# Edge-record scatters of a two-layer graph network kernel: the pacing by SyncE's answers is taken out, the pacing by TensorE's products stays

## The chip, the cores and the metric

One core of a Trainium2 chip runs the whole program in one launch. The metric is device time in microseconds, the median of three runs. PE is TensorE (its weight loads are shown as PEld), DVE is VectorE, ACT is ScalarE, POOL is GpSimd and SP is SyncE. A name with q behind it (SPq, POOLq) is the instruction queue of that engine.

## The reference, cut to what matters

Two layers work on N = 6250 nodes with 256 features and 200000 edges. Each layer adds three things to x: a sum over edges, a linear attention over all nodes, and a feed-forward part.

```python
xn = _layernorm(x)
x = x + _L0_gnn_ref(xn, src, dst, ...) + _L0_mix_ref(xn[None], ...)[0]
x = x + _L0_ffn_ref(_layernorm(x)[None], ...)[0]
xn = _layernorm(x)
x = x + _L1_gnn_ref(xn, edge_weight, W, b, src, dst) + _L1_mix_ref(xn[None], ...)[0]
x = x + _L1_ffn_ref(_layernorm(x)[None], ...)[0]
# _L0_gnn_ref: softmax-weighted sum of x[s] over the edges of each target d
# _L1_gnn_ref: segment_sum((x @ W)[edge_col] * edge_val, edge_row) + b
```

The first edge sum goes by `dst`, and the edges arrive sorted by it. The second goes by `src`, and for it the kernel has to bring the edges into another order itself.

## The kernel before

The nodes stand in 50 blocks of 125. Two blocks are a chunk, so a pass over all nodes has 25 chunks (NC = 25). The kernel runs in stages, with all engines joined between them: sort_edges (places of the edges are counted), first_layer (layer 0's norm, projections, attention), edge_softmax (layer 0's edge sum with gathers), second_layer (layer 0's feed-forward, layer 1's projections and attention), edge_sums (layer 1's edge sum with gathers), norm_and_route, and the last feed-forward part.

The second order of the edges is made by scatters. An edge is a record of three words. `Turns` writes them from SBUF to the DRAM tensor `records1`, 128 records with one indirect DMA on POOL (L585). There are 46 turns of 34 scatters, 1564 in all. A turn has two halves of SLOT = 17 scatters, and each half has its own buffer (`slot_rec`, `slot_pos`). One turn (34 scatters) runs in sort_edges, FIRST_TURNS = 18 turns (612 scatters) in first_layer, and 27 turns (918 scatters) in second_layer. In both layers the scatters run beside TensorE's work and nothing in the layer needs them. The end of the stage does: POOL waits there for all of its scatters to land.

Three waits stand ahead of a scatter:

- `filled` (L577), once for each half: SP has loaded the half's 17 columns of records and positions (L549, L550). SP issues these loads when the scatters that used this buffer before have landed (`sent[h]`).
- `beat` (L582), ahead of 21 of the 34 scatters of a turn. PE's products in first_layer and second_layer increment it, and before the loop POOL adds `lead` to it itself (L574): `Turns("a", turns, 21, 40)` in first_layer and `Turns("b", turns, 21, 50)` in second_layer. Scatter n of turn i needs a count of 21 i + floor(21 n / 34) + 1. So the scatters may run ahead of PE by 40 or 50 counts, and one count is 34/21 scatters.
- `seen` (L583), ahead of each scatter. This is the answer of SP. POOL increments `issued` ahead of each scatter (L584). SP waits in its function `follow` for each of these increments, and increments `seen` for each (L541). It starts with AHEAD = 2 answers given, so scatter j waits for the answer to scatter j - 2. SP gives the answers in the order of its own program: between them stand its waits for `sent[h]` and its issues of the loads for the next half.

first_layer runs two passes of 25 chunks on PE. In the first pass (keys, values and small projections; L774, L782, L790, L794) a chunk gives 7 counts. In the second pass (queries, messages, feed-forward; L815, L827, L840, L848) it also gives 7. L774 and L815 leave 8 matmul records for a chunk. DVE does the counting of places (`Places.blocks`, L217 to L227) during the first pass. SP may only load positions that are already spilled, and waits for `spilled[i]` between batches of turns.

second_layer begins with the selection of the top rows: BITS + 2 = 18 rounds between PE (L1175) and DVE, each a product that waits for DVE's counts and gives them back summed. Its passes then give 8 counts per chunk (feed-forward, L1200), 3 (keys, values, products; L1233) and 10 (queries and messages; L1255, L1282, L1289, L1304, L1315).

Of the kernel before, what the change touches and what calls it, by code (L numbers as in the profile page):

```python
# [35 lines left out]
LAG = 4  # L36
AHEAD = 6
RW = 3
# [6 lines left out]
SLOT = 17  # L45
# [27 lines left out]
def settle(pool, cell, settled, before):  # L73

    pool.wait_ge(settled, before)
    pool.tensor_tensor(cell, cell, cell, ALU.add).then_inc(settled, 1)  # L76
# [25 lines left out]
def gps_kernel(nc, A, out):  # L102
# [3 lines left out]
    def sem(name):  # L106

        held = nc.semaphore(name)
        phase_sems.append((held, held.__enter__()))
        return phase_sems[-1][1]  # L110
# [35 lines left out]
    with ctx:  # L146
# [376 lines left out]

        class Turns:

            AHEAD = 2

            def __init__(self, name, turns, beats=0, lead=0):
                self.at, self.turns, self.beats, self.lead = moved[0], turns, beats, lead
                self.filled = [sem(f"{name}_filled{h}") for h in range(2)]  # L530
                if beats:
                    self.beat = sem(name + "_beat")
                self.settled, self.issued, self.seen = (sem(f"{name}_{x}") for x in ("settled", "issued", "seen"))
                moved[0] += 2 * SLOT * turns

            def sp(self, sp, first, n):

                def follow(i, h, a, b):
                    with loop(sp, b - a) as j:
                        sp.wait_ge(self.issued, i * (2 * SLOT) + (h * SLOT + a + 1) + j)  # L540
                        sp.sem_inc(self.seen, 1)  # L541

                def turn(i, k):
                    for h in range(2):
                        at = self.at + first * 2 * SLOT + h * SLOT
                        cols = bass.ds(i * (2 * SLOT) + at, SLOT)
                        if not (isinstance(i, int) and self.at + first == 0):
                            sp.wait_ge(sent[h], i * (16 * SLOT) + 8 * (self.at + first * 2 * SLOT))
                        sp.dma_start(slot_rec[:, h, :, :], spill_rec[1][:, cols, :]).then_inc(self.filled[h], 16)  # L549
                        sp.dma_start(slot_pos[:, h, :], spill_pos[1][:, cols]).then_inc(self.filled[h], 16)  # L550
                        if h:
                            follow(k, 0, 4, SLOT)
                        elif not (isinstance(k, int) and k == 0):
                            follow(k - 1, 1, 4, SLOT)
                        follow(k, h, 0, 4)

                if first == 0:
                    sp.sem_inc(self.seen, self.AHEAD)
                    turn(0, 0)
                    if n > 1:  # L560
                        first = 1
                        with loop(sp, n - 1) as i:
                            turn(i, i + 1)
                        first = 0
                elif n:
                    with loop(sp, n) as i:
                        turn(i, i + first)
                if first + n == self.turns:
                    follow(self.turns - 1, 1, 4, SLOT)

            def pool(self, pool):

                if self.beats:
                    pool.sem_inc(self.beat, self.lead)  # L574
                with loop(pool, self.turns) as i:
                    for h in range(2):
                        pool.wait_ge(self.filled[h], i * 32 + 32)  # L577
                        settle(pool, cell[0:1, 0:1], self.settled, i * 2 + h)
                        for j in range(SLOT):
                            n = h * SLOT + j  # L580
                            if self.beats and (n * self.beats // (2 * SLOT) > (n - 1) * self.beats // (2 * SLOT)):
                                pool.wait_ge(self.beat, i * self.beats + n * self.beats // (2 * SLOT) + 1)  # L582
                            pool.wait_ge(self.seen, i * (2 * SLOT) + h * SLOT + j + 1)  # L583
                            pool.sem_inc(self.issued, 1)  # L584
                            pool.indirect_dma_start(  # L585
                                out=rec_d[1], out_offset=bass.IndirectOffsetOnAxis(ap=slot_pos[:, h, j:j + 1], axis=0),
                                in_=slot_rec[:, h, j, :], in_offset=None).then_inc(sent[h], 16)
                for h in range(2):
                    pool.wait_ge(sent[h], 8 * (self.at + 2 * SLOT * self.turns))
# [1300 lines left out]
        def edge_softmax(edge):  # L1890
# [4 lines left out]
            with ExitStack() as c:  # L1895
# [32 lines left out]
                with nc.Block() as block:  # L1928
# [73 lines left out]
                    def _(act):  # L2002
# [19 lines left out]
                        def body(t, s):  # L2022
                            d, x = s % 2, step(t, s)
                            if near(t, s, AHEAD):
                                step_records(act, *near(t, s, AHEAD))
                            if near(t, s, 3):
# [8 lines left out]

                        for i in range(AHEAD):
                            step_records(act, 0, i)
# [398 lines left out]
```

## Time and profile before

| | us |
|---|---|
| median of three runs | 8288.19 |
| lowest and highest run | 8277.54 and 8334.47 |
| the profiled execution | 8300.19 |
| its span | 8298.5 |
| PE busy | 5030.9 (61%) |
| POOL busy | 4735.0 (57%) |
| DVE busy | 3712.8 (45%) |
| L585, the scatters, x1564: busy | 1573.5 |
| L585: POOL idle just before them | 942.9 |

first_layer's part with scatters runs from about 200 to 1215 us of the span, second_layer's from about 3981 to 5560 us. A PE that is busy for 61% of the span isn't at its limit there, since the matmuls are pipelined. Idle time of POOL ahead of a scatter is shared out by the semaphore event that came last before it, so a wait that ended by PE's count is often shown as one for SPq L541, because SP's answer comes just behind it.

### The profile page before, as it was taken

Reading aid. Unit: us, or ns where it says so; the run is one execution under the profiler, and the core shown is the slowest. Engines: PE = TensorE matmul, PEld = TensorE weight load, DVE = VectorE, ACT = ScalarE, POOL = GpSimd, SP = SyncE. Lnnn points to the kernel's source line nnn. Section 1 sums busy time; section 2 is a strip of 40 time slices with the busy share of each in tenths; the row PEclk is TensorE's granted clock in tenths of the full one; section 3 lists DMA queues with packets and bytes.
Section 4 is the critical chain, followed back from the end, with each engine's and each line's share of the span. In section 5 each row is a group of like instructions: output and inputs, shape, how many; then the busy total and the mean of one; then the engine's idle time right before and its main releaser. Section 6 shows DMA issues by size and latency. Waiting matters only on the chain. (4 is left out here: it accounts for less than half of the span.)

```text
span 8298.5 us, 129786 instructions
## 1 busy us (share of the span) xinstructions
PE 5030.9 (61%) x23474; PEld 3877.8 (47%) x23475; DVE 3712.8 (45%) x14369; ACT 1845.1 (22%) x4706; POOL 4735.0 (57%) x5589
## 2 busy tenths in 40 slices
PE   0464666666666667776288777654445444444499
PEld 0353544545554545555266666543333333333377
DVE  6463444444555555555554424433333333333445
ACT  6111333333333333333122222210000000000044
POOL 2576646665555555555566556656666666666500
PEclk9886767787778888888689988877777777777799
DMA  3100003333333333333100000013333333333200
GB/s 87 34 4 6 3 13 89 90 89 87 84 85 84 81 81 84 82 82 80 36 3 4 20 17 3 3 32 91 91 91 91 91 91 91 91 91 92 74 25 18
DMA packets 505323, 495.45 MB, mean 60 GB/s; under 512 B 374862, under 2 KB 402135, under 8 KB 504407
## 3 DMA queue, kind: packets, MB, share of 16 engines
q0 software_dynamic: 200192, 432.72, 19.1%
q1 hardware_dynamic: 154712, 33.52, 2.2%
q10 hardware_dynamic: 150271, 27.46, 1.9%
q8 instruction: 66, 1.08, 0.1%
q14 instruction: 82, 0.67, 0.0%
HBM read 463.03 MB, written 30.23 MB: 59 GB/s over the span
## 5 line engine op out<-in xcount | busy, mean ns | idle before, releaser
L1847 POOL DMA_INDIRECT XN<-table,XN x3128 | 2984.5, 954 | 985.6 <-issue 917.4
L585 POOL DMA_INDIRECT records<-slot_rec,slot_pos x1564 | 1573.5, 1006 | 942.9 <-SPq L541 531.2
L2159 PE MATMUL gcn_psE<-XN,gcn_pE 128*125 x3520 | 1125.0, 484 | 1213.3 <-DVE gcn_pE L2175 922.9
L2159 PEld LDWEIGHTS gcn_psE<-XN,gcn_pE 128*125 128x125 f32 x3520 | 825.8, 243 | 1512.5 <-issue 1352.2
L1978 PE MATMUL gat_psE<-XN,gat_pE 128*125 x3520 | 1112.8, 470 | 190.2 <-ACT gat_pE L2034 171.2
L1978 PEld LDWEIGHTS gat_psE<-XN,gat_pE 128*125 128x125 f32 x3520 | 784.3, 234 | 351.9 <-issue 206.2
L2187 DVE TENSOR_TENSOR X<-X,gcn_psE 125x256 f32 x440 | 184.3, 419 | 1537.3 <-remote 1077.6
L76 POOL TENSOR_TENSOR cell<-cell 1x1 int32<-1x1 int32 x874 | 162.7, 186 | 1174.7 <-remote 505.4
L2241 ACT ACT_TABLE_LOAD x1 | 1.3, 1283 | 2345.0 <-PEq L118 2345.0
L1970 PE MATMUL gat_psP<-ident,XN 125*128 125x125 f32 x1760 | 325.7, 316 | 324.3 <-ACT gat_sc L2030 211.2
L2175 DVE TENSOR_SCALAR gcn_pE<-iota_n,gcn_lk,gcn_rec 128x125 f32<-128x125 f32 x1760 | 502.8, 362 | 16.0
L1970 PEld LDWEIGHTS gat_psP<-ident,XN 125*128 125x128 f32 x1760 | 241.1, 165 | 466.8 <-ACT gat_sc L2030 253.5
L2072 DVE COPY gat_mo<-edge_m 125x1 f32 x440 | 67.7, 154 | 871.2 <-remote 641.6
L1962 PE MATMUL gat_psS<-XN,gat_kTs 32*125 32x128 f32 x3520 | 255.6, 364 | 312.8 <-DVE gat_df L2078 202.7
L2061 DVE TENSOR_SCALAR gat_pen<-gat_psT,iota_p 125x512 f32<-125x512 bf16 x440 | 329.4, 749 | 172.4 <-ACT XN L2010 101.6
L2034 ACT ACTIVATE gat_pE<-gat_psP 128x500 f32<-128x500 f32 x440 | 257.8, 586 | 587.7 <-PE gat_psP L1970 283.7
L1962 PEld LDWEIGHTS gat_psS<-XN,gat_kTs 32*125 32x125 f32 x3520 | 166.5, 215 | 412.7 <-issue 245.6
L2019 ACT ACTIVATE XN<-XN 128x100 f32 x440 | 128.1, 291 | 883.1 <-issue 876.5
L2029 ACT ACTIVATE XN<-XN,gat_nm 125x512 f32<-125x512 f32 x440 | 310.8, 706 | 9.0 <-issue 9.0
L2073 DVE CUSTOM_DVE_ANT_0 XN<-gat_psS,gat_pen 125x512 f32<-125x512 f32 x440 | 304.3, 692 | 0.0
L1200 PE MATMUL b_bank<-room,b_wf 128*128 128x250 f32 x800 | 217.1, 432 | 79.3 <-ACT room L1354 46.8
L1200 PEld LDWEIGHTS b_bank<-room,b_wf 128*128 128x128 f32 x800 | 171.1, 223 | 123.8 <-ACT room L1354 51.4
(454 smaller groups left out, 8178.0 us busy)
## 6 DMA issues: line engine op xcount, KB each, us to landing
XN<-table,XN POOLq DMA_INDIRECT x3128
records<-slot_rec,slot_pos POOLq DMA_INDIRECT x1564
XN<-records SPq DMA_DIRECT2D x782, 6.0 KB
gat_rec<-records ACTq DMA_DIRECT2D x440, 6.0 KB
gcn_rec<-records ACTq DMA_DIRECT2D x440, 6.0 KB
table<-XN ACTq DMA_DIRECT2D x5, 1250.0 KB
table<-room ACTq DMA_DIRECT2D x25, 250.0 KB
out_x<-X SPq DMA_DIRECT2D x25, 250.0 KB
```

The costliest lines, as they stand in the source:

```text
L585: pool.indirect_dma_start(out=rec_d[1], out_offset=bass.IndirectOffsetOnAxis(ap=slot_pos[:, h, j:j + 1], axis=0), in_=slot_rec[:, h, j, :] ...
L1200: last = pe.matmul(psH[i % 2][:, 0:TOK], wf1[:, j, i * P:(i + 1) * P], xT[:, j, :], start=(j == 0), stop=(j == KF - 1))
L1847: pool.indirect_dma_start(out=rows_t[:, s, j, :], out_offset=None, in_=table, in_offset=bass.IndirectOffsetOnAxis(ap=rec_g[:, s, j, 1:2].b ...
L1962: last = pe.matmul(psS[0:B, j, :], kTs[r, d, :], qT[r, d, :], start=True, stop=True)
L1970: last = pe.transpose(psP[:, j * B:(j + 1) * B], pT[:, d, j * P:(j + 1) * P], ident[0:B, 0:B])
L1978: last = pe.matmul(psE[d][0:B, 0:D], pE[:, d, j * B:(j + 1) * B], rows_t[:, slot_of(g), j, 0:D].rearrange("p a w -> p (a w)"), start=(j == ...
L2029: act.activation(pT[:, d, :], S[:, d, :], ACT.Exp, bias=nm[:, d:d + 1], scale=SC, accum_out=rs[:, d:d + 1])
L2034: act.activation(pE[:, d, :], psP[:, 0:SUB * B], ACT.Copy).then_inc(p_done, 1)
L2061: dve.tensor_scalar(pen[:, d, :], psB[0:B, :], iota_p[0:B, 0:1], -BIG, ALU.not_equal, ALU.mult).then_inc(pen_done, 1)
L2073: st(dve.tensor_tensor_reduce(out=S[:, d, :].rearrange("p (j n) -> p j n", j=SUB), in0=psS[0:B, :, :], in1=pen[:, d, :].rearrange("p (j n) ...
L2159: last = pe.matmul(psE[d][0:B, 0:D], pE[:, d, j, :], rows_t[:, slot_of(g), j, :].rearrange("p a w -> p (a w)"), start=(j == 0), stop=(j == ...
L2175: last = dve.tensor_scalar(pE[:, d, j, :], iota_n[:, :], lk[:, d, j:j + 1], rec_t[:, s, j, 2:3], ALU.is_equal, ALU.mult)
```

## The change

`Turns` loses `AHEAD`, `issued`, `seen` and `follow`. SP's part of a turn is now only the wait for `sent[h]` and the two loads of each half. POOL's part keeps the waits for `filled` and `beat`. Behind each wait for `beat` (21 in a turn) it now increments a new semaphore, `paced`, that nothing waits for. The leads stay 40 and 50. sort_edges' turn has no beats, so its 34 scatters now wait for `filled` alone. Nothing else differs between the two kernels.

```diff
--- before.py
+++ after.py
@@ -523,24 +523,17 @@
 
         class Turns:
 
-            AHEAD = 2
-
             def __init__(self, name, turns, beats=0, lead=0):
                 self.at, self.turns, self.beats, self.lead = moved[0], turns, beats, lead
                 self.filled = [sem(f"{name}_filled{h}") for h in range(2)]
                 if beats:
-                    self.beat = sem(name + "_beat")
-                self.settled, self.issued, self.seen = (sem(f"{name}_{x}") for x in ("settled", "issued", "seen"))
+                    self.beat, self.paced = sem(name + "_beat"), sem(name + "_paced")
+                self.settled = sem(name + "_settled")
                 moved[0] += 2 * SLOT * turns
 
             def sp(self, sp, first, n):
 
-                def follow(i, h, a, b):
-                    with loop(sp, b - a) as j:
-                        sp.wait_ge(self.issued, i * (2 * SLOT) + (h * SLOT + a + 1) + j)
-                        sp.sem_inc(self.seen, 1)
-
-                def turn(i, k):
+                def turn(i):
                     for h in range(2):
                         at = self.at + first * 2 * SLOT + h * SLOT
                         cols = bass.ds(i * (2 * SLOT) + at, SLOT)
@@ -548,25 +541,13 @@
                             sp.wait_ge(sent[h], i * (16 * SLOT) + 8 * (self.at + first * 2 * SLOT))
                         sp.dma_start(slot_rec[:, h, :, :], spill_rec[1][:, cols, :]).then_inc(self.filled[h], 16)
                         sp.dma_start(slot_pos[:, h, :], spill_pos[1][:, cols]).then_inc(self.filled[h], 16)
-                        if h:
-                            follow(k, 0, 4, SLOT)
-                        elif not (isinstance(k, int) and k == 0):
-                            follow(k - 1, 1, 4, SLOT)
-                        follow(k, h, 0, 4)
-
-                if first == 0:
-                    sp.sem_inc(self.seen, self.AHEAD)
-                    turn(0, 0)
-                    if n > 1:
-                        first = 1
-                        with loop(sp, n - 1) as i:
-                            turn(i, i + 1)
-                        first = 0
-                elif n:
+
+                if self.at + first == 0:
+                    turn(0)
+                    first, n = 1, n - 1
+                if n:
                     with loop(sp, n) as i:
-                        turn(i, i + first)
-                if first + n == self.turns:
-                    follow(self.turns - 1, 1, 4, SLOT)
+                        turn(i)
 
             def pool(self, pool):
 
@@ -580,8 +561,7 @@
                             n = h * SLOT + j
                             if self.beats and (n * self.beats // (2 * SLOT) > (n - 1) * self.beats // (2 * SLOT)):
                                 pool.wait_ge(self.beat, i * self.beats + n * self.beats // (2 * SLOT) + 1)
-                            pool.wait_ge(self.seen, i * (2 * SLOT) + h * SLOT + j + 1)
-                            pool.sem_inc(self.issued, 1)
+                                pool.sem_inc(self.paced, 1)
                             pool.indirect_dma_start(
                                 out=rec_d[1], out_offset=bass.IndirectOffsetOnAxis(ap=slot_pos[:, h, j:j + 1], axis=0),
                                 in_=slot_rec[:, h, j, :], in_offset=None).then_inc(sent[h], 16)
```

## Rows read from the trace of the kernel before

**Rows 1.** The page: the span, PE's line, and the group of the scatters

```profile
span 8298.5 us, 129786 instructions
...
PE 5030.9 (61%) x23474; PEld 3877.8 (47%) x23475; DVE 3712.8 (45%) x14369; ACT 1845.1 (22%) x4706; POOL 4735.0 (57%) x5589
...
L585 POOL DMA_INDIRECT records<-slot_rec,slot_pos x1564 | 1573.5, 1006 | 942.9 <-SPq L541 531.2
```

**Rows 2.** Waits in 535 to 865 us, SP's and POOL's: us, times, longest

```profile
SPq L541 <- POOLq L584: 1.0, 4, 0.3
...
POOL records L585 <- issue: 53.5, 159, 2.1
POOL records L585 <- SPq L541: 51.3, 53, 4.7
```

**Rows 3.** The same waits of SP in 865 to 1180 and in 4130 to 5500 us

```profile
SPq L541 <- POOLq L584: 107.9, 94, 4.5
...
SPq L541 <- POOLq L584: 382.1, 323, 24.8
```

**Rows 4.** L585 alone by windows: stretch, length, POOL busy (scatters), PE clock, DMA, GB/s

```profile
200.00:535.00 335.00, 217.11 (x204) 0.88 0.11 27
430.00:535.00 105.00, 83.77 (x70) 0.87 0.04 5
535.00:682.00 147.00, 95.21 (x99) 0.70 0.10 8
682.00:865.00 183.00, 120.09 (x124) 0.68 0.03 3
865.00:1180.00 315.00, 182.08 (x187) 0.74 0.03 3
3970.00:4100.00 130.00, 83.82 (x81) 0.53 0.18 52
```

**Rows 5.** L774 alone by windows, PE and PEld (8 records are a chunk)

```profile
270.00:385.00 115.00, 22.47 (x48) 14.93 (x48) 0.78 0.10 24
385.00:430.00 45.00, 11.59 (x40) 8.03 (x40) 0.96 0.02 4
430.00:535.00 105.00, 23.88 (x64) 15.79 (x64) 0.87 0.04 5
535.00:665.00 130.00, 22.21 (x48) 14.91 (x48) 0.73 0.06 4
```

**Rows 6.** L815 alone by windows, PE and PEld (8 records are a chunk)

```profile
680.00:865.00 185.00, 18.45 (x64) 14.60 (x64) 0.68 0.03 3
865.00:1180.00 315.00, 35.72 (x136) 30.41 (x136) 0.74 0.03 3
```

**Rows 7.** Timelines of PE, ACT, DVE and POOL, 650 to 674 us: start, length, idle before

```profile
650.18 0.96 POOL L585 DMA_INDIRECT records<-slot_rec,slot_pos  x1 [0.30 <-issue]
651.53 2.09 PE L646 MATMUL a_bank<-room 125*128 125x129 f32 x8 [4.22 <-issue]
...
659.30 18.28 ACTq L890 DMA_DIRECT2D spill_pos<-room  x1
...
669.83 0.18 DVE L655 COPY a_kvd<-a_bank 32x32 f32<-32x32 f32 x1 [10.56 <-remote]
...
673.37 0.96 POOL L585 DMA_INDIRECT records<-slot_rec,slot_pos  x1 [3.20 <-SPq L541]
```

**Rows 8.** Timeline of PE, the 18 rounds of the selection (1st, 4th, 10th, 18th)

```profile
4058.46 0.58 PE L1175 MATMUL b_bank<-b_cnt,ones 125*125 125x3 f32 x2 [85.89 <-issue]
...
4077.01 0.58 PE L1175 MATMUL b_bank<-b_cnt,ones 125*125 125x3 f32 x2 [10.65 <-issue]
...
4097.26 0.58 PE L1175 MATMUL b_bank<-b_cnt,ones 125*125 125x3 f32 x2 [4.44 <-DVE b_tot L1476]
...
4115.12 0.58 PE L1175 MATMUL b_bank<-b_cnt,ones 125*125 125x3 f32 x2 [1.57 <-DVE b_v L1496]
```

**Rows 9.** Waits of ACT's L1403, which reads L1255's product: us, times

```profile
  remote: 120.9, 21
```

## The prediction

> **What bounds the kernel now.** The page first: PE is busy for 61% of the span, and POOL stands idle for 942.9 us ahead of its scatters, 531.2 of them put down to SP's answers [rows 1]. That is the sum the change seems to be after. Two questions come before it: did an answer end this idle time, and does anything wait for the scatters?
>
> The waits of SP and POOL, cut by stretch, answer the first. From 865 to 1180 us SP itself waits 107.9 us for POOL's `issued` [rows 3]. SP is there ahead of POOL, and what holds POOL can only be PE's count. From 4130 to 5500 us it is the same, with 382.1 us [rows 3]. From 535 to 865 us SP waits for POOL for 1.0 us in all [rows 2]. There SP is the late one and its answers hold POOL: 51.3 + 53.5 us in 212 gaps [rows 2], and with 0.30 us for a gap without a wait [rows 7] this leaves 105 - 64 = 41 us of pauses in 223 scatters.
>
> The counts say the same. By 535 us PE has done (48 + 40 + 64) / 8 = 19 chunks [rows 5], 133 counts, and with the lead 173. 204 scatters have run [rows 4], and the next needs 6 x 21 + 1 = 127. POOL has 46 counts in hand. By 865 us it has issued 427 and the next needs 12 x 21 + 11 + 1 = 264, and PE has given 175 + 8 x 7 = 231 [rows 6] and the lead 40. The hand is nearly empty, and it stays so to the last scatter. The lead in second_layer is 50 counts, 81 scatters, and 81 is what runs by 4100 us [rows 4].
>
> The second question: the scatters end before PE does in both stages, so POOL's idle time is off the path. The path is PE's chain with DVE and ACT. But the scatters press on it. At 651.53 us PE starts the last key-value sums, 2.09 us of work, and DVE, which waits for them, starts at 669.83 us, after 10.56 us of idle time [rows 7]. An issue of a DMA on ACT takes 18.28 us in the same stretch [rows 7]. Nothing of this is work. The semaphore updates of the products arrive late while POOL issues at its full rate, 0.96 + 0.30 = 1.26 us for a scatter [rows 7], and they arrive when POOL has paused for a few microseconds (here the 3.20 us ahead of 673.37 [rows 7]). The selection in second_layer measures it. Its last 8 rounds, after POOL's lead is spent, take (4115.12 - 4097.26) / 8 = 2.23 us each. The 9 rounds before that, beside the scatters, take 38.8 / 9 = 4.3 us each, and one gap in them is 10.65 us [rows 8]. Where a scatter takes longer the pressure is gone: from 430 to 535 us one comes each 1.5 us, and PE makes 8 chunks in 105 us, 13.1 us each. From 535 us on it takes 130 / 6 = 21.7 us for a chunk [rows 4, 5].
>
> **The change part by part.** Taken out on POOL: 1564 increments and waits; on SP: 1564 waits and increments. They run in the queues beside a scatter of 0.96 us and take nothing off the path. Added: 945 increments of `paced` on POOL, hidden in the same way, and at most some tens of ns each behind a beat wait if not. SP comes to its wait for `sent[h]` sooner, so the loads of the next half (two issues each) come as early as now or earlier; behind them in SP's queue only the wait for spilled positions stands, which is set by DVE.
>
> What is left is what the answers do to POOL's rhythm. An answer is a semaphore update too. When updates are late it is late as well, POOL stops, and the backlog clears. Without it POOL goes on as long as it has counts in hand, and loses nothing by PE's being late.
>
> First layer, to 385 us: POOL has few counts over; a change of some microseconds either way, taken as 0. From 385 to 535 us nothing changes, since positions and DVE set the pace. At 535 us POOL has 46 counts, 46 x 34/21 = 74 scatters, and now issues them at 1.26 us: 94 us in which PE's chain gets little done, to 629 us. From then on each scatter waits for PE's count. In this regime, 865 to 1180 us, a chunk takes 315 / 17 = 18.5 us with 11 scatters [rows 4, 6]. The 6 chunks left of the first pass take 111 us, so the pass ends at about 740 us instead of 665, and 75 us are lost. The 8 chunks of the second pass that now take 183 / 8 = 22.9 us each take 18.5, and 35 us come back. Net +40 us. Two bounds. If the waits for the buffers (one each 17 scatters) let PE do two chunks within the burst, 37 us come off: +3. If a chunk of the first pass takes 20 us and one of the second 19, the net is +94 + 120 - 130 - 31 = +53. I take +25, nearer to the middle, because the trace has no run of scatters without answers and so no row for a complete standstill.
>
> Second layer, selection: POOL's 81 scatters end some 4 us sooner. If PE stands still until then (4095 us) with 15 rounds left, these end at 4095 + 15 x 2.23 = 4128 us instead of 4115: +13. If the rounds run as now, -4. I take +8. The rest of the stage is held by counts already [rows 3], and stays: 0. The sum is 8300 + 25 + 8 = 8333 for an execution like the profiled one. This one stood 12 us over the median, so 8320 us for the median.
>
> DMA: Bandwidth & Descriptors of the Trainium skill (section Anatomy of one DMA) says that the DMA engines wait for no semaphore, and that every wait happens at the issuing sequencer. By that nothing but POOL's own waits bounds what is outstanding; the trace agrees in so far as POOL's pauses are what ends the late updates [rows 7].
>
> **The rivals.**
> *Nothing changes (chance 0.26).* The answers only follow POOL, and PE loses to the scatters what it loses to them in any rhythm: the number of scatters stays 612 and 918. For it: the time that the burst costs comes back, as the +3 above shows. It gives 8300 - 12 + 0 = 8288, from -10 to +10. SBUF: State Buffer of the Trainium skill (section SBUF: two separate sides) has a rule on this side: only GpSimd's and VectorE's shared port contends, and PE and ACT wait for no one. By it the scatters could not hold PE in any rhythm and the sum would be 0. The 10.56 and 18.28 us of idle and issue time beside dense scatters [rows 7] speak against reading it so widely, for they are no access to SBUF.
> *The bursts grow everywhere (0.16).* Slower by more than 1%. Also where counts are few, an answer now cuts a run of scatters short. ACT waits 120.9 us in 21 chunks for products of L1255 that PE has long issued [rows 9], 5.8 us each. If a run is longer by two scatters, 2.5 us, in each of the second layer's 75 chunks and the first layer's last 17, this is 92 x 2.5 = 230 us at most; with half of it on the path, and the 33 above, 8288 + 33 + 115 = 8436. It decides from 0.6 us per chunk on. Against it: SP is ahead in these stretches [rows 3], so its answers are seldom the last.
> *The answers are part of the load (0.10).* Each scatter carries two more semaphore updates and a loop of SP. Without them 1.26 us per scatter may be slow enough that no backlog forms. Then first_layer's 14 chunks between 535 and 865 us run at 18.5 us or less: 330 - 259 = 71 us saved, and the selection's 18, in all 8288 - 89 = 8199. Against it: two updates beside the landing of a DMA on 128 partitions are little.
>
> **How the numbers follow.** The forecast has 0.48: 8320 us, alone 8285 to 8350. A measurement of this kernel can tell about 1% (83 us) from no change. Slower by over 1% are the rival of growing bursts and the tail of the forecast: 0.16 + 0.02. Faster by over 1% is most of the last rival: 0.08. Within 1%: 0.46 + 0.26 + 0.02 = 0.74. The range leaves out half of each outer rival: 8255 to 8395 us.
>
> **What would show it.** In the profile after: POOL's idle ahead of L585 in 535 to 640 us falls to 0.30 us a scatter, with runs of some 17 or more. The chunks of L774 stand nearly still there, and from about 640 us on come each 17 to 20 us; L815 begins at about 740 to 760 us instead of 682. The rounds of L1175 bunch behind POOL's 81st scatter. Stages without records scatters keep their lengths. Wrong would be: L774 at its present 21.7 us or faster right through the burst (the last rival, or none), or chunks of L1255 that take longer than now (the rival of growing bursts).

## The result, and the profile after

The changed kernel takes 8331.2 us (median of 20 runs, 8307.5 to 8373.4) against 8302.7 us of the kernel before (20 runs, 8269.7 to 8334.5). The ratio is 1.0041, with a 95% interval of 1.003 to 1.0052. The medians are 28.5 us apart, and the ratio stands for 34 us. That lies inside the predicted range, and on the side that was forecast. The profiled execution spans 8331.3 us, where the one before spans 8298.5 us [rows 1].

Of the four sets of experiments three ran where the kernel before takes 8297, 8380 and 8308 us, and one where it takes 6696 us, so every ratio below is against the kernel before within its own set. The kernel before has a trace only from the first measurement; where a stage of it is named below without a set, it is from that trace.

The lines behind the class Turns stand 20 lines higher than before: L585 is now L565, L774 is L754, L815 is L795, L1175 is L1155, L1255 is L1235, L1403 is L1383.

The page after, its span, PE's line and the group of the scatters, which answer to [rows 1]:

```profile
span 8331.3 us, 121212 instructions
...
PE 4994.7 (60%) x23474; PEld 3863.2 (46%) x23475; DVE 3712.0 (45%) x14369; ACT 1847.5 (22%) x4706; POOL 4736.6 (57%) x5589
```

```profile
L565 POOL DMA_INDIRECT records<-slot_rec,slot_pos x1564 | 1569.1, 1003 | 971.3 <-issue 421.7 <-PE b_bank L1262 158.3 <-remote 108.3
```

The answers' 531.2 us are gone from the list, and the idle time is still there, 28 us longer. Other releasers have taken it over. On the whole it was not the answers that kept POOL idle. Whether an answer ended a single run of scatters is another question, and the second layer answers it below.

First layer. PE's L754 by windows of the profile after (8 records are a chunk), to be held against [rows 5]:

```profile
535.00:573.00 38.00, 0.31 (x2) 0.22 (x2) 0.63 0.04 3
573.00:656.00 83.00, 3.51 (x9) 2.55 (x10) 0.54 0.03 3
656.00:762.00 106.00, 16.70 (x40) 11.04 (x39) 0.73 0.12 9
```

POOL's waits in 535 to 656 us, and L565 by windows (length, POOL busy, scatters):

```profile
POOL records L565 <- issue: 31.6, 84, 2.0
```

```profile
535.00:762.00 227.00, 140.38 (x145) 0.64 0.08 6
762.00:1180.00 418.00, 259.21 (x263) 0.78 0.03 3
```

POOL issues 86 scatters in 121 us with 84 gaps of 0.38 us, and from 573 to 656 us PE gets little more than one chunk done. That is the standstill of the forecast. Then 5 chunks take 106 us, 21 each. All of it comes back in the second pass. PE's L795 by its first and last start, after:

```profile
L795 PE MATMUL a_bank<-room,a_wq x200: 372/374/784, 762.0 to 1177.6; 128*128 128x250 f32 x100
```

and the same line of the kernel before, L815:

```profile
L815 PE MATMUL a_bank<-room,a_wq x200: 372/374/784, 681.9 to 1179.8; 128*128 128x250 f32 x100
```

The pass starts 80 us later and ends 2 us sooner. Second layer, the first and last round of the selection (L1155) and the query pass (L1235), after:

```profile
L1155 PE MATMUL b_bank<-b_cnt,ones x36: 349/361/372, 4080.8 to 4119.1; 125*125 125x3 f32 x36
L1235 PE MATMUL b_bank<-room x200: 372/374/784, 4845.2 to 5489.9; 128*128 128x250 f32 x100
```

and before:

```profile
L1175 PE MATMUL b_bank<-b_cnt,ones x36: 349/361/372, 4058.5 to 4115.4; 125*125 125x3 f32 x36
L1255 PE MATMUL b_bank<-room x200: 372/374/784, 4858.7 to 5455.8; 128*128 128x250 f32 x100
```

Gathers stand on both sides of the layer. L1827 (L1847 before) by its first and last start, in edge_softmax and in edge_sums, after:

```profile
L1827 POOL DMA_INDIRECT XN<-table,XN x1564: 943/949/994, 1220.5 to 3927.4; - x196
L1827 POOL DMA_INDIRECT XN<-table,XN x1564: 945/949/1076, 5567.8 to 7877.6; - x196
```

and before:

```profile
L1847 POOL DMA_INDIRECT XN<-table,XN x1564: 942/949/994, 1222.8 to 3943.6; - x196
L1847 POOL DMA_INDIRECT XN<-table,XN x1564: 941/949/1074, 5533.6 to 7842.2; - x196
```

So first_layer ends 2 us earlier, edge_softmax is 14 us shorter (2707 against 2721), edge_sums is the same (2310 against 2309), and second_layer takes 1640 us instead of 1590. Inside it the selection's first round comes 153 us after the last gather, before 115, and its rounds take 38 us, before 57: together +20. The query pass takes 645 us, before 597: +48. The two passes between give back 17.

These are differences of single profiles. In the four profiles in which first_layer runs with its answers the first gather comes at 1213.6 to 1231.2 us, so a difference of a few us says nothing. The 14 us of edge_softmax are outside what five other profiles show (2721 to 2729 us), and no run explains them.

What late looks like. Timeline of the profile after in the query pass (start, length, engine, idle before):

```profile
5204.76 1.85 PE L1235 MATMUL b_bank<-room 128*128 128x250 f32 x8
...
5206.46 0.65 PE L613 MATMUL b_bank<-ident,room 125*128 125x125 f32 x4
...
5211.54 0.59 ACT L1383 ACTIVATE room<-b_bank 128x500 f32<-128x500 f32 x1 [5.13 <-remote]
...
5212.87 0.68 DVE L1569 SCALAR_TENSOR_TENSOR room<-b_bank,room 128x500 f32<-128x500 f32 x1 [7.51 <-ACT room L1385]
...
5216.47 0.59 ACT L1389 ACTIVATE room<-b_bank 128x500 f32<-128x500 f32 x1 [3.69 <-remote]
...
5217.20 1.07 PE L613 MATMUL b_bank<-ident,room 125*128 125x125 f32 x4 [10.09 <-issue]
...
5222.33 0.96 POOL L565 DMA_INDIRECT records<-slot_rec,slot_pos  x1 [6.65 <-PE b_bank L1262]
```

ACT's L1383 reads the query products (L1235). They are done by 5206.6 us, ACT is free from 5206.4 on, and it starts at 5211.5. L1389 reads the transposes (L613). They are done by 5207.1 us, and L1389 starts at 5216.5, 3.7 us after ACT is free. The other counts that these two wait for are of earlier chunks. What waits for ACT is in time here: DVE's L1569 starts 0.09 us behind the end of L1385, and PE's second transposes start 0.14 us behind the end of L1389. From one group of transposes to the next 10.7 us pass. PE's timeline gives a median of 10.7 us for this step over the pass and 8.7 us in the kernel before. All this time POOL issues a scatter each 1.26 us, nine in a row from 5204.6 to 5214.7.

It is not only what waits for another engine that is late. PE's timeline of the profile after, in the standstill of first_layer (start, length, idle before):

```profile
611.96 0.38 PE L626 MATMUL a_bank<-room 125*128 125x129 f32 x1 [1.73 <-issue]
614.76 0.38 PE L626 MATMUL a_bank<-room 125*128 125x129 f32 x1 [2.42 <-issue]
617.56 0.38 PE L626 MATMUL a_bank<-room 125*128 125x129 f32 x1 [2.42 <-issue]
```

These are three of the eight records of one call of `kv_sums`, and the kernel has no wait between them. At 539.81 us all eight take 1.06 us together. Here they start 2.1 to 3.5 us apart, as the transposes ahead of them do. The prediction and the expectations speak of late semaphore updates. That names what a waiting engine sees. Whether updates arrive late, or instructions are handed to the engines late, or both, no run separates, and "late" in what follows leaves it open.

### The profile page after: what moved, and what is told of

It reads as the page before. It is cut to its first block and busy times, and to the rows that moved or that the text cites. A ratio compares the mean times of both kernels' runs of the same rounds, so it can differ in the third digit from the quotient of the medians.

```text
span 8331.3 us, 121212 instructions
## 1 busy us (share of the span) xinstructions
PE 4994.7 (60%) x23474; PEld 3863.2 (46%) x23475; DVE 3712.0 (45%) x14369; ACT 1847.5 (22%) x4706; POOL 4736.6 (57%) x5589
## 5 line engine op out<-in xcount | busy, mean ns | idle before, releaser
L1827 POOL DMA_INDIRECT XN<-table,XN x3128 | 2987.7, 955 | 991.7 <-issue 925.1
L565 POOL DMA_INDIRECT records<-slot_rec,slot_pos x1564 | 1569.1, 1003 | 971.3 <-issue 421.7
```

What stands on the lines that cost most here:

```text
L565: pool.indirect_dma_start(out=rec_d[1], out_offset=bass.IndirectOffsetOnAxis(ap=slot_pos[:, h, j:j + 1], axis=0), in_=slot_rec[:, h, j, :] ...
L1827: pool.indirect_dma_start(out=rows_t[:, s, j, :], out_offset=None, in_=table, in_offset=bass.IndirectOffsetOnAxis(ap=rec_g[:, s, j, 1:2].b ...
```

## The experiments

Two theories went into them. **Places:** updates come late while POOL issues back to back. An answer is an update too, so when things are late it stops POOL. That is worth something only where POOL would otherwise have to wait for PE later. **Fixed cost:** a scatter costs the others a fixed time in any rhythm, and the answers add to it or not. In the experiments Turns takes a range of turns, `answered`, in which SyncE's answers are kept as before; their lines stand some 15 lower than those of the kernel before.

### Which part of the kernel the loss sits in (one set; before 8297 us)

**First layer alone without answers.**

```diff
-mv = Turns("a", turns, 21, 40)
+mv = Turns("a", turns, 21, 40, answered=None)        # given up
-mv = Turns("b", turns, 21, 50)
+mv = Turns("b", turns, 21, 50, answered=(0, 99))     # kept
```

> Answers of SyncE given up in the head and in first_layer (19 of the 46 turns of 34 scatters), kept in all 27 turns of second_layer. The output is complete. Theory of places (the cost is made in second_layer, and the burst of first_layer gives back in its second pass what it took): first_layer's scatters run as without answers, a standstill of 70 to 90 us from 573 us on, the first gather at 1220 to 1223 us, and the whole within 5 us of the kernel before (ratio 0.999 to 1.001). The prediction's own term for this stage, +25 us: ratio 1.003. A third theory, that the answers cost or save something per scatter wherever they stand: 0.41 of the change's +33 us, +14 us, ratio 1.0016.

Measured: ratio 0.9999, 0.9982 to 1.0016. Its second pass, as above:

```profile
L830 PE MATMUL a_bank<-room,a_wq x200: 372/374/784, 757.7 to 1185.5; 128*128 128x250 f32 x100
```

The standstill is there (the pass starts at 758 us), and the first gather comes at 1224 us. The layer loses nothing that can be seen, and the prediction's +25 us is outside the interval, if narrowly (1.003 against 1.0016). The third theory's 1.0016 lies on its edge and isn't decided here.

**Second layer alone without answers** (`answered` the other way round).

> Answers given up in second_layer alone. Theory of places: second_layer takes 1630 to 1645 us from the last gather of one layer to the first of the next (before 1590), the whole +30 to +51 us, ratio 1.0035 to 1.006. The prediction's own term for this stage, +8 us: ratio 1.001. A cost per scatter: 0.59 of +33 us, +19 us, ratio 1.0023.

Measured: ratio 1.0056, 1.0035 to 1.0077. second_layer takes 1628 us, the query pass 642 us. The whole loss of the change sits in this layer. The prediction's 1.001 and the 1.0023 of a cost per scatter are outside the interval.

**Its first 3 turns alone** (`answered=(3, 99)` for "b", all other turns answered).

> Answers given up in the first 3 of second_layer's 27 turns alone: the 81 scatters of the lead, beside the selection, and 21 more. Theory of places: first round of the selection +40 us, the rounds themselves -19 us, so second_layer +21 us and the passes behind it as before: ratio 1.0025. If what the selection loses is made up by the passes behind it: ratio 1.000. If the run of scatters without an answer is all that matters and it is worst here: as much as the whole change, ratio 1.004 or more.

Measured: ratio 1.0035, 1.0021 to 1.0048; second_layer 1608 us. Selection and query pass:

```profile
L1190 PE MATMUL b_bank<-b_cnt,ones x36: 349/360/373, 4105.5 to 4143.8; 125*125 125x3 f32 x36
L1270 PE MATMUL b_bank<-room x200: 372/374/784, 4878.6 to 5475.4; 128*128 128x250 f32 x100
```

First round 159 us after the last gather (3946.4), rounds in 38 us, query pass 597 us as before. The selection's loss stands alone: +18 us of the layer in the profiles. The ratio's interval holds both the first line's 1.0025 and the last line's 1.004; it is the profile, with the passes behind the selection as before, that speaks for the first.

**Its turns 15 to 26 alone** (`answered=(0, 15)`).

> Answers given up in turns 15 to 26 of second_layer alone, which are those beside the query pass (4860 to 5450 us), in which few counts are in hand. Theory of places, with the mechanism of the rival of growing bursts: the query pass takes 640 us (before 595), the selection, the feed-forward and the key-value pass as before; ratio 1.005 to 1.006. If the query pass of the changed kernel was late only for what the burst at the start left behind: it takes 595 us, ratio 1.000.

Measured: ratio 1.0038, 1.0022 to 1.0055; second_layer 1615 us.

```profile
L1190 PE MATMUL b_bank<-b_cnt,ones x36: 349/360/373, 4066.3 to 4123.9; 125*125 125x3 f32 x36
L1270 PE MATMUL b_bank<-room x200: 372/374/787, 4866.2 to 5489.7; 128*128 128x250 f32 x100
```

The selection is as before (first round after 113 us, rounds in 58) and the query pass takes 623 us, +26 of the +48, less than the 640 us expected. That part of the loss is made in the pass itself and is no remainder of the burst at the start. The other 22 us come only when the turns ahead of 15 go without answers too (642 us in the run with the whole layer so), and they don't come with the first 3 turns alone. What carries them over wasn't settled.

### Where nothing is late (one set; before 6696 us)

In this set the lateness doesn't exist, so its runs don't test the theories, which are about a kernel of 8300 us. They show what the kernel is without it.

**One scatter ahead of the answer instead of two** (`AHEAD = 1`), and **eight** (`AHEAD = 8`).

> The kernel before with all its answers, but each scatter waits for the answer to the scatter just ahead of it, not to the one before that. If an answer is of use because it is itself an update that comes late, and so ends a dense run: runs end one scatter earlier, 1.3 us for each run; query pass 575 to 595 us, whole ratio 0.997 to 1.000. If the answers hold GpSimd on the whole too tightly and the burst's scatters are only pushed into the passes behind it: ratio 1.000 to 1.003.

> The kernel before with all its answers, but GpSimd may be eight scatters ahead of them instead of two. The answers are still sent, so what they cost stays; only the length of a run until a late answer ends it changes. If the pause is what counts: between before and the changed kernel, nearer to the changed one, since a run of 10 scatters is 12.6 us: query pass 615 to 645 us, ratio 1.002 to 1.004. If the updates that SyncE and GpSimd exchange were what mattered (a load that keeps the rest in order): as before, ratio 1.000.

Measured: 1.0002 (0.9993 to 1.0011) and 1.0 (0.9991 to 1.0009). Neither theory said this, for both spoke of a kernel of 8300 us. The timeline of the query pass with `AHEAD = 1`, the same instructions as in the fence above:

```profile
3788.00 0.65 PE L648 MATMUL b_bank<-ident,room 125*128 125x125 f32 x4
3788.06 0.59 ACT L1418 ACTIVATE room<-b_bank 128x500 f32<-128x500 f32 x1
...
3789.39 0.68 DVE L1604 SCALAR_TENSOR_TENSOR room<-b_bank,room 128x500 f32<-128x500 f32 x1 [2.50 <-ACT room L1420]
...
3789.92 0.62 PE L648 MATMUL b_bank<-ident,room 125*128 125x125 f32 x4 [1.27 <-ACT room L1424]
```

L1418 reads the products here 0.04 us after their end, not 4.9 us. The first transposes, ACT's and DVE's instructions are as long as in the changed kernel above (0.65, 0.59, 0.68 us; a scatter 0.96 + 0.30), and POOL issues as densely. The second transposes are not: 0.62 us here, 1.07 there, where PE had stood idle for 10.09 us. These are the two levels of TensorE's clock. The granted clock over the query pass is 0.99 here and 0.82 in the kernel of 8300 us. From transposes to transposes 1.9 us pass, there 10.7, and the median over the pass is 2.1 us. The query pass takes 406 us instead of 597:

```profile
L1270 PE MATMUL b_bank<-room x200: 372/374/784, 3696.5 to 4102.3; 128*128 128x250 f32 x100
```

Dense scatters and lateness are thus two things: in this set the first is there without the second.

**The scatters of second_layer started when the selection is done** (`pool.wait_ge(sel_done, 1)` ahead of `mv.pool(pool)`).

> The kernel before with its answers, but GpSimd starts the records of second_layer only when the selection is done. Where the burst of 81 scatters runs is all that changes. The selection then takes 38 us for its 17 rounds at 2.2 us and its first round comes 80 to 100 us after the last gather: it ends 50 to 65 us earlier. If a burst costs what it costs wherever it stands: the feed-forward pass is longer by the same 50 to 65 us, ratio 0.999 to 1.001. If the burst is worse beside the passes, in which TensorE stands nearly still for 81 x 1.26 = 102 us: the pass longer by about 100 us, ratio 1.004 to 1.006. If the passes behind it give the time back as first_layer's second pass does: ratio 0.993 to 0.997.

Measured: 1.0152, 1.0138 to 1.0166; second_layer 1356 us instead of the 1255 of the run with `AHEAD = 1`. None of the three ranges holds this. The layer is 101 us longer, which looks like the 102 us of the second line and isn't: the passes take as long as with `AHEAD = 1` (feed-forward 341 and 342 us, query pass 409 and 406). Here POOL is the bound of the layer: its last scatter starts 17 us ahead of the next stage's first gather (4247 and 4264 us with `AHEAD = 1`), so a start 111 us later (3146 against 3035) is passed on nearly whole. What this does in the other condition wasn't tried.

**The changed kernel with an addition of 128x128 on POOL ahead of each scatter.**

```diff
+pool.wait_ge(self.padded, ...)
+pool.tensor_tensor(pad[:, :], ones[:, 0:128], ones[:, 0:128], ALU.add).then_inc(self.padded, 1)
 pool.indirect_dma_start(
```

> The changed kernel, with an addition of 128x128 on GpSimd into a tile that nobody reads ahead of each record scatter of both layers: about 0.45 us, so one scatter each 1.55 to 1.65 us instead of 1.26 in a dense run. No answers. Theory that the updates come late because scatters are issued back to back: the standstill of first_layer's first pass (573 to 656 us) is gone, the selection's first round starts some 110 us after the last gather (154 in the changed kernel, 114 before), the query pass takes 595 us or less, and the whole is at or below the kernel before, ratio 0.99 to 1.000. Theory that each scatter costs the others a fixed time at any rhythm: ratio of the changed kernel, 1.003 to 1.005. Theory that GpSimd's time becomes the bound (308 scatters x 1.6 = 493 us of 595 in the query pass, 306 x 1.6 = 490 of 481 us in the feed-forward pass): the feed-forward pass longer by 10 us or more, ratio above 1.005.

Measured: 1.0764, 1.075 to 1.0779, 512 us more. Over the 1530 scatters of both layers that is 0.33 us each, and one scatter comes each 1.58 us in its timeline instead of 1.26: what the addition puts between them is passed on whole. The feed-forward pass itself is no longer than with `AHEAD = 1` (342 us both); the layers end later because POOL does. It says nothing on lateness, since there was none.

### The rhythm, where things are late (one set; before 8380 us)

**The changed kernel once more**, as the companion of the two others.

> The changed kernel as it stands. The four runs before these fell on a chip on which the kernel before takes 6696 us instead of 8297, with every instruction as long as here but the waits for semaphores short. Theory that the change costs time only where the updates come late: on a chip of 6696 us the ratio is 0.999 to 1.001, on one of 8300 us 1.003 to 1.006, as in the first measurement. Theory that the longer runs of scatters themselves cost time (their load on the memories and queues): 1.003 or more on either.

Measured: 1.0079, 1.0065 to 1.0092. That is more than in the first measurement (1.0041), and the kernel before is slower too (8380 against 8303 us). With two sets that is no rule.

**All answers sent, but POOL may be 34 scatters ahead of them** (`AHEAD = 34`).

> The kernel before with all its answers sent, but GpSimd may be 34 scatters ahead of them instead of two, so that they hardly ever hold it. Theory that the pause is what an answer is worth: as the changed kernel on the same chip (8300 us: ratio 1.003 to 1.006, standstill in the first pass, query pass 640 us; 6696 us: 1.000). Theory that the updates exchanged between GpSimd and SyncE matter by themselves: as the kernel before, 1.000, on a chip of 8300 us.

Measured: 1.0085, 1.0071 to 1.0099, as the changed kernel beside it. With the traffic of the answers still there and their hold on POOL loosened, the loss of the whole is the same, and 1.000 is excluded. So the exchange of updates isn't what kept the kernel before ahead. The shape is not the same: first_layer's first pass takes 424 us, as in the changed kernel (435), but the selection's rounds take 59 us as before and the query pass 607 us instead of the 640 expected, while the first round comes 132 us after the last gather. In the query pass the runs of scatters are as short as in the kernel before (4.4 scatters on average, before 4.3, changed 5.0, counted in POOL's timeline; a run goes on while starts are no more than 1.45 us apart). So that the pause is all that an answer is worth isn't shown for the query pass. Where this run loses its time is open, since the kernel before has no trace in this set.

**The changed kernel with an addition of 128x96 ahead of each scatter.**

> The changed kernel with an addition of 128x96 on GpSimd into a tile that nobody reads ahead of each record scatter: one scatter each 1.5 to 1.6 us in a dense run instead of 1.26. Theory that the updates come late because scatters are issued back to back, on a chip of 8300 us: no standstill of the first pass, the selection's first round 110 us after the last gather, the query pass 595 us or less, ratio at or below 1.000. Theory that each scatter costs the others a fixed time at any rhythm: 1.003 to 1.005. On a chip of 6696 us GpSimd is the bound of both layers: 1564 x 0.27 = 420 us more, ratio 1.06.

Measured: 0.9874, 0.9857 to 0.989, the first version ahead of both kernels. POOL's timeline in second_layer:

```profile
4850.02 0.99 POOL L606 DMA_INDIRECT records<-slot_rec,slot_pos  x1 [0.17 <-issue]
4851.04 0.35 POOL L605 TENSOR_TENSOR pad<-ones 128x96 f32<-128x96 f32 x1
4851.55 0.99 POOL L606 DMA_INDIRECT records<-slot_rec,slot_pos  x1 [0.16 <-issue]
```

One scatter each 1.53 us, without a pause, or 1.58 with the waits for loads, as L606 alone shows for the query pass (259 in 409 us):

```profile
4791.00:5200.00 409.00, 259.78 (x259) 0.99 0.03 3
```

And this is what it does to PE:

```profile
L795 PE MATMUL a_bank<-room x200: 377/379/791, 278.3 to 528.9; 128*125 128x256 f32 x100
L1276 PE MATMUL b_bank<-room x200: 372/374/784, 4791.1 to 5200.0; 128*128 128x250 f32 x100
```

The first pass takes 251 us (before 363, after 435) and the query pass 409 us (before 597, after 645). In the set of 6696 us they take 242 and 406 us. With 0.3 us more from scatter to scatter the lateness is gone from these passes. The run did not simply meet the other condition: its edge_softmax, whose gathers have no addition, takes 2765 us, in the changed kernel beside it 2745 and in the set of 6696 us 1980. The theory of a fixed cost falls. Whether it is the time between two scatters or the other instruction in it that helps, no run separates. Much of the gain is not cashed in because POOL is now the bound of both layers: its scatters run to 5477 us, 277 us behind PE's last chunk. The engines also wait ahead of the query pass, as DVE's line shows:

```profile
DVE b_nshift L1595 <- DMA spill_pos<-room: 113.5, 1, 113.5
```

SyncE stores the last positions only behind the loads of turn 14, and those wait for POOL's scatters to land.

### A version that goes on from there (one set; before 8308 us)

**Shorter additions, and ahead of the gathers too:** 128x32 in first_layer and both edge stages, 128x48 in second_layer.

> The changed kernel with a shorter addition on GpSimd ahead of each indirect DMA, of the gathers too: 128x32 in first_layer and in both edge stages (about 1.40 us for one DMA in a dense run, where it was 1.26), 128x48 in second_layer (1.43). Where the kernel before takes 8300 to 8400 us: if the updates are in time again from 1.40 us on, every stage is bound by GpSimd or by its own work: first gather at about 1100 us, edge_softmax 1564 x 1.42 = 2220 us (before 2721), second_layer 1330 to 1430 us (before 1590), edge_sums 2220 us (before 2308), the whole 7300 to 7500 us, ratio 0.87 to 0.90. If 1.40 us is still too dense: chunks as late as in the kernel before, edge_softmax 2650 us or more, ratio 0.98 to 1.01. A difference between the two layers (1.40 against 1.43 us) would say where the limit lies. Where the kernel before takes 6700 us: GpSimd is the bound of four stages, 4692 x 0.15 = 700 us more, ratio 1.09 to 1.11.

Measured: 0.9678, 0.9653 to 0.9702, 8048 us. PE's passes and the gathers:

```profile
L795 PE MATMUL a_bank<-room x200: 377/379/788, 274.6 to 524.3; 128*125 128x256 f32 x100
L1276 PE MATMUL b_bank<-room x200: 372/374/783, 4625.0 to 5055.2; 128*128 128x250 f32 x100
L1871 POOL DMA_INDIRECT XN<-table,XN x1564: 960/966/999, 1147.7 to 3839.0; - x196
L1871 POOL DMA_INDIRECT XN<-table,XN x1564: 962/966/1077, 5291.5 to 7592.3; - x196
```

The whole missed both ranges. The layers came near to what was expected: first gather at 1148 us (expected about 1100, before 1223), second_layer 1452 us (expected 1330 to 1430, before 1590). The scatters alone (L606), beside the second pass of first_layer (590 to 980 us) and in the query pass:

```profile
590.00:980.00 390.00, 264.65 (x267) 0.79 0.03 3
4625.00:5055.00 430.00, 288.22 (x289) 0.95 0.03 3
```

So a scatter comes each 1.46 and 1.49 us, not each 1.40 and 1.43 as expected, for some of them take longer beside other work. The query pass takes 430 us, a little more than at 1.58 (409); the first pass is still free (250 us). The edge stages did not do what was expected: edge_softmax takes 2691 us instead of 2220, and edge_sums 2301 us instead of 2220. The gathers come in fours, 1.40 us apart, with a wait for PE behind them, 1.72 us each over the stage. Whether their neighbours stay late because 1.40 is too dense within a group, or because this stage is late for another reason, is open.

## Why the prediction was right, and where it wasn't

**The size was right by cancellation, which is luck.** The steps gave +25 in first_layer, +8 in the selection and 0 in the rest of second_layer. The profiles have -2, +20 and +30, and the runs in which one part alone goes without answers bear this out (0.9999; 1.0035; 1.0038). The step from 8333 to 8320 us leaned on a median of three runs. Over 20 runs the median of the kernel before is 8302.7 us, so the profiled execution stood 2 us under it and not 12 over, and the sum of +33 would have given 8336 us.

**What bounds it: right on the whole.** The answers' 531.2 us vanished and POOL stayed idle as long, and the counts in hand at 535 us, 46 counts or 74 scatters, did run off in one burst.

**First layer: the mechanism and the loss right, the return mis-sized.** The first pass was to end at about 740 us and ended at 762; the loss was set at 75 us and is 80. The return was set at 35 us, from 8 chunks that would run at 18.5 us, while the 17 behind them stayed as they were. It is 82 us: 25 chunks took 416 us, 16.6 each. The rate per chunk did not carry over. Counted by scatters it does: before, 99 + 124 + 187 = 410 scatters take 645 us from 535 to 1180 us [rows 4], and after, 145 + 263 = 408 take the same 645 us, 1.58 each. What is issued in the burst is missing later, so chunks come faster. This is a reading of two profiles and no law: within the stretch the kernel before has a scatter each 1.48 us (682 to 865) and each 1.68 us (865 to 1180), and in the query pass the time for one grows from 1.62 to 1.75 us. The step that failed is "+25, nearer to the middle", with the return of 35 us as its mis-sized term. The bound of +3 was near the right value, but not for its own reason, two chunks done within the burst: there was little more than one. The reason stands in the first rival.

**Selection: right in kind, mis-sized.** +8 was taken from a range of -4 to +13, and it is +20. The rounds bunch behind the burst, as said, and gain 19 us. But the step looked at the rounds alone. Ahead of them stand 50 products of DVE, which are late beside the burst too: from the first to the last start they take 66 us, before 27.5, and the first round comes 38 us later. DVE's wait ahead of L1438 in 3960 to 4100 us, after:

```profile
DVE room L1438 <- remote: 30.3, 14, 3.1
```

Before, the same wait (L1458) is 5.6 us in 3 pieces. The upper bound was too low, because it priced only those instructions of the stage of which a row was shown.

**Rest of second_layer: wrong.** "The rest of the stage is held by counts already, and stays: 0" is the step that failed. SyncE's waits for POOL [rows 3] showed that its answers were seldom the late ones on the whole; they didn't show that an answer never ended a run. POOL's waits in the query pass, 4845 to 5490 us after:

```profile
POOL records L565 <- PE b_bank L1262: 145.2, 35, 8.2
POOL records L565 <- issue: 89.8, 272, 2.0
POOL records L565 <- remote: 30.5, 23, 2.9
```

Before, the list is led by the answers, 139.0 us in 97 pieces; now 35 pieces of 145.2 us for PE. In POOL's timeline the 368 scatters of the pass stand in 86 runs before (4.3 scatters each) and in 73 after (5.0 each). Fewer pauses, each longer, and 1.9 us more for each of the 25 chunks. That is the rival of growing bursts, with its place and mechanism, at 48 us instead of the 115 that it was given, and with runs longer by 0.7 scatters instead of two. It had said that it decides from 0.6 us a chunk. In first_layer's last 17 chunks it did not show.

**The other rivals.** That nothing changes holds for first_layer, with its very reason. That the answers are part of the load, and that things go faster without them, falls with the result: the changed kernel sends none and is slower, by as much as the run with `AHEAD = 34`, which sends them all, beside it (1.0079 and 1.0085). The rule of the Trainium skill on SBUF (SBUF — State Buffer, section SBUF: two separate sides), by which PE and ACT contend with no one there, agrees with the set of 6696 us, in which PE and ACT are not late beside dense scatters (1.9 us from transposes to transposes). The lateness of the other sets (10.7 us) is no access to SBUF that a trace shows.

**The mechanism.** That dense scatters make the others late, and that scatters further apart don't, is borne out by the run with 128x96. That it is "the semaphore updates of the products" that arrive late was argued and isn't shown: the 18.28 us of an issue on ACT [rows 7] and the matmuls of L626 without a wait between them, 2.1 to 3.5 us apart, are no waits for a product. The prediction's own example reads the other way too. DVE starts at 669.83 us, and POOL's pause of 3.20 us ahead of 673.37 begins only at 670.17 [rows 7], so it isn't this pause that let DVE go on, and the rows don't bear out that the trace agrees there with the Trainium skill on what POOL's waits bound.

## What to carry to other kernels

Where one engine issues indirect DMAs back to back, look at how long after a product's end its reader starts, and at how that changes with the rhythm of the issues. If it is late by microseconds (4.9 us in the timeline above), a small piece of useless work between two issues can be worth more than it costs (0.9874 here), and where it isn't, such a piece is pure loss (1.0764, with 128x128). A handshake that seems to hold an engine for 531 us may cost nothing, and its removal is to be priced by the run of issues that it allows, and over every instruction that stands beside that run. Here a count of issues came nearer than a rate of chunks in first_layer, and neither would have given the query pass.

## What the runs showed of the hardware that was not expected

The same program takes 6696 us in one set and 8297, 8380 and 8308 us in the others, with the instructions of ACT, DVE and POOL as long in both. In the sets of 8300 us things are late beside dense indirect DMAs: from transposes to transposes a median of 8.7 us in the kernel before, and 2.1 us in the set of 6696 us (there with `AHEAD = 1`). PE's matmuls run at the lower level of its clock more of the time: the median record of L774 takes 0.63 us, and 0.38 us in the set of 6696 us, with granted clocks of 0.80 and 0.88 over the kernel. That is the smaller part. In the query pass PE is busy for 417 us before and for 372 us in the run with 128x96, so the clock stands for at most 45 of the 188 us between 597 and 409. The sets of 6696 and 8380 us ran on a chip of the same number, so it doesn't look like a lasting property of one chip; what sets it is open. Over these sets the lateness is steep in the rhythm of the scatters. In runs of one each 1.26 us, cut by pauses, the query pass takes 597 to 645 us; at a steady one each 1.49 us it takes 430, at 1.58 us 409, and 406 where nothing is late. The Trainium skill says that the record of such a DMA on GpSimd ends when its descriptors are made and not when the data has moved (Perfetto Trace Analysis, section DMA Instruction — SWDGE (GPSIMD)). That fits records of 0.96 us that stay the same in every condition, while the harm beside them comes and goes: 191 us in one pass (597 against 406).
